# Similarity bias off TensorE, a paired last eviction, and a reordered tail in a one-core attention kernel

## The reference, cut to what matters

```python
# 1. cross attention of h = layernorm(x) over ctx
Sim = (h @ w1)[:, None] + (ctx @ w2)[None, :] + (h * w3) @ ctx.T + b_sim      # 128 x 12544
A = softmax(Sim, axis=1)
hq_hat = A @ ctx
Batt = softmax(Sim.max(axis=1))
hc_hat = broadcast(Batt @ h)
x = x + concat([h, hq_hat, h * hq_hat, h * hc_hat]) @ W_qv + b_qv
# 2. linear attention (no softmax), 16 heads of 16, rotary q and k
h = layernorm(x)
q, k, v = rope(h @ Wq + bq), rope(h @ Wk + bk), h @ Wv + bv
x = x + ((q @ k.T / 4) @ v) @ Wo + bo                                         # per head
# 3. feed forward with a shift by one token
h = layernorm(x); prev = h shifted down by one row, first row zero
xr = mu_r * h + (1 - mu_r) * prev;  xk = mu_k * h + (1 - mu_k) * prev
x = x + sigmoid(xr @ W_r) * (square(relu(xk @ W_k)) @ W_v)
```

## Time and profile before

| | us |
|---|---|
| median of three runs | 113.96 |
| the profiled execution | 114.25 |
| its span | 112.4 |
| TensorE busy | 106.4 |
| VectorE busy | 93.7 |
| ScalarE busy | 80.7 |
| GpSimd busy | 20.1 |

### The profile page before, as it was taken

How to read it: one execution, slowest core, us unless ns; L and a number is a source line. 1 busy time by engine, 2 the same in 40 slices (tenths; PEclk the granted TensorE clock), 3 DMA queues, 4 the chain that set the end, 5 groups by cost and what they waited for, 6 DMA issues and landing times.

```text
span 112.4 us, 1827 instructions
## 1 busy us (share of the span) xinstructions
PE 106.4 (95%) x579; PEld 84.8 (75%) x579; DVE 93.7 (83%) x152; ACT 80.7 (72%) x169; POOL 20.1 (18%) x41
## 2 busy tenths in 40 slices
PE   5999999999999999999999999999999998998790
PEld 2458667665657587899989999898898997887480
DVE  1576998998999999979999999999999947674342
ACT  5067573889969975799999899989986625912350
POOL 2142000000000004224233323367240000200100
PEclk9999999999999999999999999999999999999999
DMA  3999999999999999999999999970000000000001
GB/s 91 356 328 413 420 420 420 420 420 420 423 410 417 418 418 417 420 392 378 370 381 408 420 420 420 420 308 1 0 6 0 0 6 0 0 0 0 6 3 47
DMA packets 8220, 29.82 MB, mean 265 GB/s; under 512 B 1042, under 2 KB 1298, under 8 KB 8082
## 3 DMA queue, kind: packets, MB, share of 16 engines
q1 hardware_dynamic: 8064, 29.69, 66.5%
q10 hardware_dynamic: 146, 0.01, 0.1%
HBM read 29.57 MB, written 0.13 MB: 264 GB/s over the span
## 4 chain that ended last, share of the span: by engine, by line
PE 55%; DMA 25%; DVE 9%; ACT 4%; issue 4%; SPq 1%; DVEq 0%; ACTq 0%
PE mixed_ps L972 18%; DMA raw<-keys_dram 17%; PE mixed_ps L974 9%; PE scores_ps L943 9%; DMA raw<-rows_dram 8%; DVE pair L676 5%; DVE neg_scores L698 3%; PE scores_ps L954 3%; ACT pair L473 2%; PE scores_ps L1065 2%; PE mixed_ps L1117 1%; PE side_ps L991 1%; PE scores_ps L1130 1%; PE side_ps L1108 1%; PE scores_ps L991 1%
## 5 line engine op out<-in xcount | busy, mean ns | idle before, releaser
L676 DVE TENSOR_TENSOR pair<-raw,pair 128x1024 fp32r<-128x1024 f32 (+1 forms) x40 | 49.3, 1244 | 2.3 <-ACT pair L473 2.2
L473 ACT ACTIVATE pair<-raw 128x512 fp32r<-128x512 f32 (+1 forms) x40 | 32.4, 810 | 8.1 <-DMA raw<-keys_dram 6.2
L972 PE MATMUL mixed_ps<-pair,turned_high 128*128 128x512 f32 x84 | 32.3, 418 | 0.0
L448 POOL CAST pair<-raw 128x512 fp32r<-128x512 f32 x22 | 13.6, 620 | 59.1 <-DMA raw<-rows_dram 34.9
L974 PE MATMUL mixed_ps<-pair,turned_low 128*128 128x256 f32 x84 | 23.6, 281 | 0.0
L972 PEld LDWEIGHTS mixed_ps<-pair,turned_high 128*128 128x128 f32 x84 | 15.8, 188 | 2.8
L505 ACT ACTIVATE turned_high<-scores_ps 128x512 fp32r<-128x512 f32 (+1 forms) x23 | 13.5, 586 | 4.3 <-PE scores_ps L943 4.3
L698 DVE TENSOR_SCALAR_CACHE_REDUCE neg_scores<-scores_ps,neg_max 128x1024 f32<-128x1024 f32 (+2 forms) x14 | 16.0, 1146 | 0.4
L974 PEld LDWEIGHTS mixed_ps<-pair,turned_low 128*128 128x128 f32 x84 | 16.0, 190 | 0.0
L705 DVE TENSOR_TENSOR turned_low<-scores_ps,turned_high 128x512 fp32r<-128x512 f32 (+1 forms) x23 | 15.3, 668 | 0.2 <-ACT turned_high L505 0.2
L943 PE MATMUL scores_ps<-ident,neg_scores 128*128 128x128 f32 x98 | 14.6, 272 | 0.0
(11 more groups left out here) (188 smaller groups left out, 120.3 us busy)
## 6 DMA issues: line engine op xcount, KB each, us to landing
raw<-keys_dram SPq DMA_DIRECT2D x24, 512.0 KB, 11.1
raw<-rows_dram SPq DMA_DIRECT2D x24, 512.0 KB, 8.8
w<-weights_dram SPq DMA_DIRECT2D x1, 1792.0 KB, 9.8
w<-weights_dram SPq DMA_DIRECT2D x2, 512.0 KB, 12.2
const<-const_dram SPq DMA_DIRECT2D x1, 832.0 KB, 11.3
raw<-keys_last_dram SPq DMA_DIRECT2D x1, 256.0 KB, 9.6
raw<-rows_last_dram SPq DMA_DIRECT2D x1, 256.0 KB, 6.6
x_sb<-x_dram SPq DMA_DIRECT2D x1, 128.0 KB, 2.1
```

The costliest lines, as they stand in the source:

```text
L473: nc.scalar.activation(pair[:, use % PAIR_BUFS, 0, 0:columns], raw[:, slot(item), 0:columns], ACT.Copy)\
L676: nc.vector.tensor_tensor(out=pair[:, use % PAIR_BUFS, 1, 0:columns], in0=raw[:, slot(item), 0:columns], in1=pair[:, use % PAIR_BUFS, 0, 0 ...
L972: nc.tensor.matmul(mixed_ps[:, :].rearrange("p (h d) -> p h d", h=2), probs_high, both[:, :, t * D:(t + 1) * D], start=(k == EARLY and t = ...
```

## The change

Four edits stand in it.

1. The bias of the similarities: `w1` and `b_sim` are loaded as one row repeated on 128 partitions (`w1_rows`, 128 x 257 floats) by the issue that loaded `bias`. GpSimd multiplies `normed` with it, ScalarE sums the products along the row after chunk 8, and VectorE adds `b_sim` when it forms `sim_max`. The six TensorE instructions after chunk 1 go.
2. Chunks 22 and 23 are evicted by one instruction.
3. V is projected ahead of K, and VectorE makes v ahead of the rotated k. The turn of q moves between the two halves of the product with Wo.
4. The shift by one token is made by TensorE: GpSimd prepares a shifted identity and the identity less the shifted one, VectorE scales both, TensorE makes `prev` and `h - prev` by two products per half in place of one, ScalarE copies `prev`, and VectorE forms `prev + mu * (h - prev)` once for k and once for r.

```diff
--- before
+++ after
-    evictions = [(k, k + 1) for k in range(0, CHUNKS - 3, 2)] + [(k,) for k in range(CHUNKS - 3, CHUNKS)]
+    evictions = [(k, k + 1) for k in range(0, CHUNKS - 1, 2)] + [(CHUNKS - 1,)]
...
+        next_token = sb("next_token", [P, P])
+        same_less_next = sb("same_less_next", [P, P])
-        bias = sb("bias", [1, 1])
+        w1_rows = sb("w1_rows", [P, D + 1])
+        hw1_parts = sb("hw1_parts", [P, D])
+        hw1_sum = sb("hw1_sum", [P, 1])
...
-        mu_left = sb("mu_left", [P, 2 * DH])
-        rstd_diagonal = neg_scores[:, 26 * D:26 * D + P]
+        to_next = neg_scores[:, 26 * D:26 * D + P]
+        to_step = neg_scores[:, 26 * D + P:27 * D]
+        prev_t = sb("prev_t", [P, DH, P])
...
-        x2n_ps = (banks[0][:, 0:P], banks[5][:, 0:P])
+        prev_ps = (banks[0][:, 0:P], banks[5][:, 0:P])
+        step_ps = (banks[3][:, 0:P], banks[4][:, 0:P])
...
 (GpSimd)
             power(0)
+            nc.gpsimd.memset(next_token[:, :], 0.0).then_inc(next_zeroed, 1)
+            pool.wait_ge(next_zeroed, 1)
+            nc.gpsimd.affine_select(out=next_token[:, :], in_=next_token[:, :], compare_op=ALU.not_equal, fill=1.0,
+                                    base=1, pattern=[[-1, P]], channel_multiplier=1).then_inc(shifts_set, 1)
+            pool.wait_ge(shifts_set, 1)
+            nc.gpsimd.tensor_tensor(out=same_less_next[:, :], in0=ident[:, :], in1=next_token[:, :], op=ALU.subtract)\
+                .then_inc(shifts_set, 1)
             pool.wait_ge(b_mean_done, 1)
...
-            nc.gpsimd.tensor_scalar(mu_left[:, :], vec[:, VC_MUR:VC_MUR + 2 * DH], -1.0, 1.0,
-                                    ALU.mult, ALU.add).then_inc(mu_left_done, 1)
+            pool.wait_ge(normed_done, DH)
+            pool.wait_ge(w1_rows_loaded, 16)
+            nc.gpsimd.tensor_tensor(out=hw1_parts[:, :], in0=normed[:, :], in1=w1_rows[:, 0:D], op=ALU.mult)\
+                .then_inc(hw1_multiplied, 1)
...
 (ScalarE)
-            act.dma_start(bias[:, :], bias_in).then_inc(bias_loaded, 16)
+            act.dma_start(w1_rows[:, :], w1_rows_in).then_inc(w1_rows_loaded, 16)
...
                 if k == 8:
                     center_x()
+                    act.wait_ge(hw1_multiplied, 1)
+                    nc.scalar.activation(hw1_parts[:, :], hw1_parts[:, :], ACT.Copy, accum_out=hw1_sum[:, :])\
+                        .then_inc(hw1_done, 1)
...
             for a in range(DH):
-                act.wait_ge(x2n_turned, a + 1)
-                nc.scalar.activation(xk_t[:, a, :], x2n_ps[a], ACT.Copy, scale=vec[:, VC_MUK + a:VC_MUK + a + 1])\
-                    .then_inc(xk_scaled, 1)
+                act.wait_ge(prev_turned, a + 1)
+                nc.scalar.activation(prev_t[:, a, :], prev_ps[a], ACT.Copy).then_inc(prev_copied, 1)
...
-            for a in range(DH):
-                act.wait_ge(xk_done, a + 1)
-                nc.scalar.activation(xr_t[:, a, :], x2n_ps[a], ACT.Copy, scale=vec[:, VC_MUR + a:VC_MUR + a + 1])\
-                    .then_inc(xr_scaled, 1)
...
 (VectorE)
-            nc.vector.tensor_tensor(out=sim_max[:, :], in0=hw1_ps, in1=neg_max[:, EVICTIONS:EVICTIONS + 1],
-                                    op=ALU.subtract).then_inc(sim_max_done, 1)
+            nc.vector.scalar_tensor_tensor(sim_max[:, :], hw1_sum[:, :], w1_rows[:, D:D + 1],
+                                           neg_max[:, EVICTIONS:EVICTIONS + 1], ALU.add, ALU.subtract)\
+                .then_inc(sim_max_done, 1)
...
             dve.wait_ge(rstd_done, 2)
+            dve.wait_ge(v_projected, 1)
+            nc.vector.scalar_tensor_tensor(v, v_ps, ln_rstd[:, 1:2], bv_rows, ALU.mult, ALU.add).then_inc(v_done, 1)
             dve.wait_ge(k_rows_projected, 1)
             rope(0, k_ps)
-            dve.wait_ge(v_projected, 1)
-            nc.vector.scalar_tensor_tensor(v, v_ps, ln_rstd[:, 1:2], bv_rows, ALU.mult, ALU.add).then_inc(v_done, 1)
             rope_sum(0)
...
             dve.wait_ge(rstd_done, 3)
-            nc.vector.tensor_scalar(rstd_diagonal[:, :], ident[:, :], ln_rstd[:, 2:3], None, ALU.mult)\
-                .then_inc(diagonal_done, 1)
-            dve.wait_ge(mu_left_done, 1)
-            for mixed_t, left, scaled, done in ((xk_t, DH, xk_scaled, xk_done), (xr_t, 0, xr_scaled, xr_done)):
+            dve.wait_ge(shifts_set, 2)
+            nc.vector.tensor_scalar(to_next[:, :], next_token[:, :], ln_rstd[:, 2:3], None, ALU.mult)\
+                .then_inc(to_next_done, 1)
+            nc.vector.tensor_scalar(to_step[:, :], same_less_next[:, :], ln_rstd[:, 2:3], None, ALU.mult)\
+                .then_inc(to_step_done, 1)
+            for mixed_t, col, done in ((xk_t, VC_MUK, xk_done), (xr_t, VC_MUR, xr_done)):
                 for a in range(DH):
-                    dve.wait_ge(scaled, a + 1)
-                    nc.vector.scalar_tensor_tensor(mixed_t[:, a, 1:P], x2n_ps[a][:, 0:P - 1],
-                                                   mu_left[:, left + a:left + a + 1], mixed_t[:, a, 1:P],
+                    dve.wait_ge(prev_copied, a + 1)
+                    dve.wait_ge(x2n_turned, a + 1)
+                    nc.vector.scalar_tensor_tensor(mixed_t[:, a, :], step_ps[a], vec[:, col + a:col + a + 1], prev_t[:, a, :],
                                                    ALU.mult, ALU.add).then_inc(done, 1)
...
 (TensorE)
-                if k == 1:
...
-                    for a in range(DH):
-                        nc.tensor.matmul(hw1_ps, normed_t[:, a, :], vec[:, VC_W1 + a:VC_W1 + a + 1],
-                                         start=(a == 0), stop=False)
-                    nc.tensor.matmul(hw1_ps, ones[0:1, :], bias[0:1, 0:1],
-                                     start=False, stop=True).then_inc(hw1_done, 1)
...
-            project(k_ps, WB_K, 0)
+            project(v_ps, WB_V, 0)
...
-            project(k_ps, WB_K, 1).then_inc(k_rows_projected, 1)
-            for out_ps, block_row, done in ((v_ps, WB_V, v_projected), (q_ps, WB_Q, q_projected)):
+            project(v_ps, WB_V, 1).then_inc(v_projected, 1)
+            for out_ps, block_row, done in ((k_ps, WB_K, k_rows_projected), (q_ps, WB_Q, q_projected)):
...
                 nc.tensor.matmul(attn_ps[a], vk[:, a, :], wo_c[:, a, :], start=True, stop=True).then_inc(attn_summed, 1)
-            pe.wait_ge(rotated_done, 2)
-            for a in range(DH):
-                nc.tensor.transpose(q_turn_ps[a], rotated[:, 1, a * P:(a + 1) * P], ident[:, :])\
-                    .then_inc(q_rot_turned, 1)
+                if a == 0:
+                    pe.wait_ge(rotated_done, 2)
+                    for b in range(DH):
+                        nc.tensor.transpose(q_turn_ps[b], rotated[:, 1, b * P:(b + 1) * P], ident[:, :])\
+                            .then_inc(q_rot_turned, 1)
...
             pe.wait_ge(x2_c_done, 1)
-            pe.wait_ge(diagonal_done, 1)
-            for a in range(DH):
-                nc.tensor.matmul(x2n_ps[a], x2_c[:, a * P:(a + 1) * P], rstd_diagonal[:, :], start=True, stop=True)\
+            pe.wait_ge(to_next_done, 1)
+            for a in range(DH):
+                nc.tensor.matmul(prev_ps[a], x2_c[:, a * P:(a + 1) * P], to_next[:, :], start=True, stop=True)\
+                    .then_inc(prev_turned, 1)
+            pe.wait_ge(to_step_done, 1)
+            for a in range(DH):
+                nc.tensor.matmul(step_ps[a], x2_c[:, a * P:(a + 1) * P], to_step[:, :], start=True, stop=True)\
                     .then_inc(x2n_turned, 1)
...
-        "bias": a["L0_xattn_b_sim"].reshape(1, 1),
+        "w1_rows": np.tile(np.concatenate([a["L0_xattn_w_sim"][0:D], a["L0_xattn_b_sim"]])[None], (P, 1)),
```

More of the change, by code:

```diff
@@ L55, with build @@
 C_MASK, C_COS, C_SIN, C_BK, C_BV, C_COS_T, C_SIN_T, C_ALL = 0, *(P + D * n for n in range(7))
-def build(nc, x, keys_in, keys_last_in, rows_in, rows_last_in, weights_in, vec_in, bias_in, const_in, out):
+def build(nc, x, keys_in, keys_last_in, rows_in, rows_last_in, weights_in, vec_in, w1_rows_in, const_in, out):
     keys_full = keys_in.rearrange("(k p) n -> k p n", p=P)
@@ L209, in build @@
         batt_ps = banks[5]
-        hw1_ps = mixed_ps[:, 0:1]
         b_mean_ps = banks[4][:, 0:D]
@@ L233, in build @@
         vec_loaded = sem("vec_loaded")
-        bias_loaded = sem("bias_loaded")
+        w1_rows_loaded = sem("w1_rows_loaded")
         w_qv_loaded = [sem(f"w_qv_loaded{n}") for n in range(2)]
@@ L277, in build @@
         total_done = sem("total_done")
+        hw1_multiplied = sem("hw1_multiplied")
         hw1_done = sem("hw1_done")
@@ L291, in build @@
         mean_const_done = sem("mean_const_done")
-        mu_left_done = sem("mu_left_done")
         x_c_done = sem("x_c_done")
@@ L341, in build @@
         x2_done = sem("x2_done")
-        diagonal_done = sem("diagonal_done")
+        next_zeroed = sem("next_zeroed")
+        shifts_set = sem("shifts_set")
+        prev_turned = sem("prev_turned")
+        prev_copied = sem("prev_copied")
```

(14 more changed lines are left out.)

## The result

The median of 20 runs is **114.44 us**, against 113.69 for 20 runs of the kernel before. The ratio is 1.0063, 95% interval 1.0038 to 1.0088, so the loss is 0.72 us (0.43 to 1.0). The forecast was 0.28 faster. The time lies in the range (112.9 to 114.6) and within 1%, but the sign is wrong.

What follows compares the result with a forecast made beforehand. Key transfers were taken to bound the first 45 us, matmuls the rows to 91, hand-overs the tail. Terms +0.31 + 0 - 0.26 - 0.33 = -0.28 us, laid on the median of 113.96, gave 113.7 us; range 112.9 to 114.6.

Steps and rivals of the forecast that it cites:

- Part 1, bias and load: Keys, up to about 45 us: the 131.6 KB load delays every later load by 0.31 us; the other added work costs nothing.
- It lands on the path whole: End of the keys part: the load's 0.31 us delays ScalarE's split at 43.97 and TensorE's start at 45.23 in full.
- Part 2, paired eviction: End of the keys part: VectorE ends 0.22 us earlier, the bank's 0.53 delay is hidden behind ScalarE's copy; value 0.
- Part 3, v first and q early: Tail: V ahead of K and q turned between the output product's halves gain 0.26 us, 0.43 if K does not delay VectorE.
- v first: Tail: what v gains is lost to a wait for K; the four matmuls end at 99.77 instead of 99.72.
- q early: Tail: the final product's first half runs beside ScalarE's second copy, so it ends at 102.58 against 102.84.
- The wait for K: Tail: the keys' rotation starts after K, so VectorE's second operation, before at 97.62, slips by 0.17 us.
- Part 4, shift: Tail: VectorE's first addition starts at 105.81 instead of 106.14, gain 0.33 us, if the unexplained wait does not return.
- The rival in which the wait stays: Tail: the unexplained 0.48 us wait before VectorE's first addition remains, giving 114.0 us; chance 0.25.
- The slow load: Start of the load stream: the 128 short rows take the engines for 1.22 us, delaying every later load; 114.6 us, chance 0.13.

## Why the prediction was wrong, step by step

**Part 1, bias and load: this is the step that failed.** The prediction said: "every later load lands later by what these bytes take. At 420 GB/s that is 0.31 us." It looked at the bytes of the new load and never at where its tile pushes the others. The row of 1028 bytes takes 1056, and with the other small tiles the ring ends up 32 bytes off. From then on each of the loads into the ring, some 16 MB from 5 to 45 us and not 0.13, moves at about 409 in place of 419 GB/s. The 0.73 us worked out above for 30 us of it compare with 0.73 to 0.93 between the means of the traces, and with 1.0048 to 1.0091 in time (0.5 to 1.0 us) for a pad that does nothing else. The changed kernel with the ring back has 0.9989 where the change has 1.0063. That accounts for the loss.

A second premise does not hold in general: "It lands on the path whole". It was read from the one trace of before, where the loads end last. In nine of eleven traces with the ring on a multiple of 256 TensorE's own work ends last before the mixing, so a small delay of the loads need not show there. ScalarE's split of the last early rows came 0.53 later (44.50 against 43.97) where 0.31 was forecast; against a typical execution of before it would be more, since the recorded one was itself behind (346 GB/s from 5 to 10 us).

The bytes themselves stay unresolved: 1.0033 (0.9988 to 1.0079) for the load placed last, with mixing at 44.85, inside the scatter. 0.31 is neither shown nor excluded; the trace of that run is one of the nine.

The work on GpSimd and ScalarE did cost nothing: the product took 0.74 (the bounds were 0.61 and 1.17), the sum 0.40, and a stall of 1.74 for a key transfer follows it where the earlier trace rows has 2.07.

The Trainium skill's page "DMA: Bandwidth & Descriptors", section "How a descriptor splits into AXI transactions", was cited in the prediction for the short rows only. What it says of a piece that does not start on a 256-byte boundary, that its first transaction starts at the boundary below and the bytes fetched for nothing cost beats, bears on the 4 KB rows of the ring as well. By it such a row takes 17 transactions in place of 16; counted in its beats of 32 bytes, an estimate is 129, 130 and 132 in place of 128 for 32, 64 and 128 bytes past the boundary, so 0.8, 1.6 and 3.1% more. The runs agree with the boundary as far as it was tested (32, 64 and 128 bytes past it all lose, 0 does not), and not with that growth: 409, 410 and 410 in place of 419, 2.1 to 2.4% less. The page speaks of bytes fetched and does not say whether it holds for the side that is written; here the source stayed the same and only the destination moved. For the rows of 1028 bytes that rule gives five transactions each, wherever they start on a multiple of 4 bytes; the prediction had five or six.

**Part 2, paired eviction: right in the trace.** The eviction took 1.28 at 43.68, mixing still followed ScalarE's copy (45.13 + 0.49), and alone the edit is 1.0002 (0.9968 to 1.0035). Its runs at full clock are 0.4 faster than those of before; whether that is the shorter tail of its trace (14.85), which the edit does not touch, is not shown.

**Part 3, v first and q early: forecast -0.26, measured +0.04** (ScalarE's first piece to the means: 95.24 to 103.30 is 8.06, before 94.82 to 102.84 is 8.02). The two halves:
- v first was put at +0.05 by itself (99.77 against 99.72). From ScalarE's first piece to the opening of the sum it took 100.38 - 95.24 = 5.14, before 99.72 - 94.82 = 4.90: +0.24. The wait for K is the 0.17 of the forecast. The missing 0.19 is the dependent pair on VectorE: a distance from start to start of 0.58 in place of 0.39. The prediction moved v out from between two instructions and did not ask what it had covered there. So v first is a loss by itself, 0.28 over the tail, and 1.0051 in time (0.31 us at full clock).
- q early was put at -0.31 and gave -0.24 alone and -0.20 behind v first (100.38 to 103.30 is 2.92, before 3.12). The mechanism is the forecast one, the wait for ScalarE's second copy included (at 102.11); the size is 0.07 short alone, and 0.11 behind v first.

**Part 4, shift: right in the trace.** VectorE's first addition comes 106.29 - 103.30 = 2.99 after the start of the means, before 3.30: -0.31, forecast -0.33. The rival in which the wait stays does not hold for the new code in any of its five traces (2.98 or 2.99). Yet one trace of the old code shows it without its wait and then just as fast, and the timed ratio of the edit alone is 0.9995 (0.9957 to 1.0033). How often the old code waits in runs without a profile is open, and so is what makes it wait.

**The rivals.** The slow load gave 114.6, close to the 114.44 measured, and would have been right by luck: it put 1.22 us at the beginning, while the second and third slices move no less than before, and the loss builds up over the whole stream. That the time fell inside the forecast range is luck too, since the term that moved it was not in the sum. The unexplained wait staying gave 114.0; it did not stay. No rival held that the other transfers would run at another rate.

The sum as it should have stood, an estimate from the traces: +0.73 to +0.93 for the ring, 0 for the eviction, +0.04, -0.31, together +0.46 to +0.66 on the median; measured +0.72 (0.43 to 1.0).

## What to carry to other kernels

Where transfers set the pace, a tile added ahead of their destination is an edit of those transfers: put odd-sized tiles behind the large buffers, or check that each destination still starts on a multiple of 256 bytes (here 48,896 and 49,920 were fast). Compare the rate of the stretch that the transfers bound before looking at any single wait. And before moving an instruction out of a chain on one engine, look at whether the two that it leaves side by side depend on each other.

## What the runs showed of the hardware that was not expected

- Rows of 4 KB written into SBUF at a start 32, 64 or 128 bytes past a multiple of 256 move at 409 to 410 GB/s, at two multiples 1024 bytes apart at 418 to 419, with the same busy share of the DMA engines (1.03). The engines' own tiles moved by 32 bytes at no cost that shows (0.9990, 0.9951 to 1.0029).
- On VectorE an addition of 128x256 that reads the result of the instruction right before it starts 0.58 after that one's start, an independent one 0.39 to 0.40.
- An unedited hand-over between ScalarE and VectorE took 0.83 to 0.84 in ten traces and 0.47 in the eleventh. No run here tells why.
- TensorE's granted clock was at the lower level (0.50) for about 3 us in the tail of two traces (of before again, and of the pad behind the ring), with tails of 16.15 and 16.08 us in place of 15.21. By the clock on record for timed runs it occurs in 44 of 236 runs with the old place of the turn of q, and in none of 68 with the new one. What makes it fall is not shown.
